# Moving the SBUF addresses of a two-layer kernel's matmul operands to multiples of 2048 bytes

## The chip, the cores and the metric

The kernel runs on one core of one Trainium2 chip. The metric is the device time of one execution in microseconds (us). Three runs of the kernel before took 1174.01, 1175.48 and 1177.17 us; the median is 1175.48 us.

## The reference

1,024 tokens of 512 channels pass two layers, in float32. With `ln` for a layer norm without weights:

```python
xn = ln(x)
x  = x + s4_convolution(xn) + W_down(silu(xn @ W_gate.T) * (xn @ W_up.T))     # 1,376 hidden
xn = ln(x)
x  = x + causal_attention(xn, 32 heads of 128, sequences of 256) @ wo \
       + (xn @ W_base.T + b_base + gated_low_rank_experts(xn))
```

Attention multiplies q and k, masks, takes a softmax over the keys, multiplies by v and projects with wo. It is by far the largest part.

## The kernel before, in words

**Arithmetic.** Float32 accuracy comes from splitting each operand into two float32r tensors, `_hi` and `_lo`. `matmul3` (lines 97 to 101) issues three matmuls into one accumulator: hi by hi (L99), stationary hi by moving lo (L100), stationary lo by moving hi (L101). The first operand of `nc.tensor.matmul` after the output is the stationary one, whose 128 columns are loaded as weights; the second one is moving, up to 512 columns streamed past them. The profile writes the moving operand first: `banks<-xT_hi,wqk_hi` streams `xT_hi` past the weights `wqk_hi`. A stationary slice is 512 bytes of a partition, a moving slice of 512 columns is 2,048.

**Layer 0** (`layer0`, about the first 283 us): `gate_up` runs the gate and up projections in units of 12 matmuls (4 slices of the channels, three matmuls each), weights `gu`, moving `xT`, 22 units for each half of the tokens; `down` has `hT` stationary and `wd` moving; `convolve` has `xT` stationary and `toep` moving; `linear` has `xT` stationary and `wc` moving; `experts` has `hwT` and `wb`. During the first half DVE also computes the convolution's kernel between its tiles, and PE waits for it in places.

**Layer 1** (`attention`, from about 283 us): eight groups of four heads. The order of PE's work is written out in the lists `GROUP` and `LAST_GROUP` and every engine follows it. Its steps: `Q` and `K` (`project`) are one unit of 12 matmuls of 512 columns each, `wqk` stationary, `xT` moving; `V` (`values_or_output`) is such a unit with `xT` stationary and `wv` moving; `W` (in the last group `A` and `B`, 9 and 3 matmuls) has `oT` stationary and `wo` moving; `S` is the scores (L1179 and a `matmul3` of 256 columns, `qT` by `kT`); `T` is three transposes of `prob` (L1188), `O` is `v` by `pT` (256 columns) and L1203. Most Q and K units stand alone between small steps: S, T, unit, O. A group ends with eight W units, seven of them in a row, and begins with S, Q, K. POOL splits the weights (L984, L986) and scales the probabilities (L1002, L1004); ACT and DVE empty the accumulators.

By these lists there are 128 Q and K units: 86 alone after a T, 16 that open a group as the pair Q, K, 8 that follow such a lone unit directly, 16 behind a V unit, 2 issued ahead. There are 64 V units: 38 alone after a T, 24 right behind another V unit, 2 issued ahead.

**Placement.** `place` (line 1224) allocates SBUF tensors one after another at the next multiple of 32 bytes, with no other rule; `late` and `early` blocks are freed and their room used again by what follows. `acc` begins at byte 16,512 of each partition. From the shapes in `build` (lines 1233 to 1261) the first bytes follow; what is left of them modulo 2048 is:

```
acc, xT_hi, xT_lo, ident                                  128
oT, wo, wc_hi, hT, gu, wd, work, toep_hi                  320
qT, kT, v, q_full, k_full, v_full, p_full, pT             320
wc_lo 480; wb, s4, hwT 640; toep_lo 832
wqk_stage, wvo_stage, wqk, wv, prob, tab                 1344
```

(`_hi` and `_lo` alike where not told apart.) Slices inside a tensor begin at multiples of 512 bytes beyond that, except in `wc`, whose rows are 2,600 bytes.

Of the kernel before, what the change touches and what calls it, by code (L numbers as in the profile page):

```python
# [18 lines left out]
P = 128  # L19
F32 = mybir.dt.float32  # L20
# [21 lines left out]
ER = NE * RANK  # L42
WC = DM + ER + NE + 2
CUT = 384
EPS = 1e-5
NEG = -1e30
MAX_THRESHOLD, SCALING = 0.125, 2.0
# [60 lines left out]
def layer0(nc, sem, shared, ins, ffn_sb, expert_sb, small_sb):  # L108
# [77 lines left out]
    def linear_bank(n):  # L186

        return G + 2 * (n % 2) if n < NT - 2 else D + 2 * (n % 2)
# [113 lines left out]
    def scalar_program(act, ahead):  # L302
# [24 lines left out]
        def hg_copy(tiles):  # L327
            for n in tiles:
                half, t = n // TH, n % TH
                act.wait_ge(base_done, n + 1)  # L330
                if half:
                    act.wait_ge(hw_done, 1)
                nc.scalar.activation(hg[:, t, :], banks[:, linear_bank(n) + 1, DM - CUT:WC - CUT],
                                     ACT.Copy).then_inc(hg_done, 1)
# [41 lines left out]
    def vector_program(dve, ahead):  # L376
# [19 lines left out]
        def variance(tiles):  # L396
# [3 lines left out]
            js = slice(tiles[0] % TH, tiles[-1] % TH + 1)  # L400
            nc.vector.tensor_scalar(ln[:, 0, js], mv[:, js, 1], EPS, None, ALU.add).then_inc(var_done, 1)

# [196 lines left out]
        def linear_add(n):  # L599
# [3 lines left out]
            dve.wait_ge(bias_added, n + 1)  # L603
            nc.vector.tensor_tensor(acc[:, t, 0:CUT], acc[:, t, 0:CUT], banks[:, bank, 0:CUT], ALU.add)
            nc.vector.tensor_tensor(acc[:, t, CUT:DM], acc[:, t, CUT:DM], banks[:, bank + 1, 0:DM - CUT],
                                    ALU.add).then_inc(base_added, 1)
# [95 lines left out]
    def tensor_program(pe, ahead):  # L702
# [45 lines left out]
        def linear(n):  # L748
# [5 lines left out]
            if 2 <= n < NT - 2:  # L754
                pe.wait_ge(base_added, n - 1)
            for b, part in ((bank, slice(0, CUT)), (bank + 1, slice(CUT, WC))):
                for k in range(KD):
# [107 lines left out]
def attention(nc, sem, shared, ins, late_sb, attention_sb):  # L865
# [5 lines left out]
    acc, xT_hi, xT_lo, ident, _, banks, y_done = shared  # L871
    w_qk, w_v, w_o, mask_dram, out = ins
    oT_hi, oT_lo, wo_hi, wo_lo = late_sb
    (qT_hi, qT_lo, kT_hi, kT_lo, v_hi, v_lo, q_full, k_full, v_full, p_full, wqk_stage, wvo_stage, wqk_hi, wqk_lo,
     wv_hi, wv_lo, prob, pT_hi, pT_lo, mask, top, total, inv) = attention_sb
    G, S, T, O = 0, 4, 6, 7

    mask_loaded = sem("mask_loaded")
# [342 lines left out]
def build(nc, x, w_gu, w_down, lam, p_ri, q_ri, ct, vc, bp, d_skip, log_step, om_rows, om_cols, tables,  # L1221
          w_comb, b_base, b_thr, w_expb, w_qk, w_v, w_o, identity, mask, out):
    with ExitStack() as ctx:
        def place(stack, *tensors):
            return [stack.enter_context(nc.sbuf_tensor(name, shape, dt)) for name, shape, dt in tensors]

        def split(name, shape):
            return (f"{name}_hi", shape, F32R), (f"{name}_lo", shape, F32R)

        def sem(name):  # L1230
            return ctx.enter_context(nc.semaphore(name))

        acc, xT_hi, xT_lo, ident = place(ctx, ("acc", [P, NT, DM], F32), *split("xT", [P, KD, TOK]),
                                         ("ident", [P, P], F32))
        small_sb = place(ctx, ("vcs", [NS, 2 * NS], F32), ("bps", [NS, NS], F32), ("sm", [NS, 12], F32),
                         ("ex", [NS, 4], F32), ("exi", [NS, 1], mybir.dt.int32), ("bb", [NS, 8], F32),
                         ("vv", [NS, 16], F32), ("omc", [P, 2, KD], F32), ("cs", [P, 12, KD], F32),
                         ("A", [P, KD, 8], F32), ("dsk", [P, 2], F32), ("st", [P, TH, 6], F32),
                         ("mv", [P, TH, 2], F32), ("ln", [P, 4, TH], F32), ("gt", [P, 10, TH], F32))


        with ExitStack() as late:
            late_sb = place(late, *split("oT", [P, GH, TOK]), *split("wo", [P, GH, DM]))
        shared_bytes = 4 * 2 * (GH * TOK + GH * DM)
        expert_bytes = 4 * (2 * KD * WC + 2 * DM + 8 * DM + 2 * TH * P)
        expert_sb = place(ctx, *split("wc", [P, KD, WC]), *split("wb", [P, DM]), ("s4", [P, 8, DM], F32),
                          *split("hwT", [P, TH, P]), ("rest", [P, (shared_bytes - expert_bytes) // 4], F32))
        with ExitStack() as early:
            ffn_sb = place(early, *split("hT", [P, NF, HALF]), ("gu_stage", [P, 2, 2, KD, P], F32),
                           *split("gu", [P, 2, 2, KD, P]), ("wd_stage", [P, 2, DM], F32), *split("wd", [P, 2, DM]),  # L1250
                           ("work", [P, 4, DM], F32), *split("toep", [P, P + DM]),
                           ("tab", [P, KD * WC + DM], F32))
        attention_sb = place(ctx, *split("qT", [P, BATCH, P]), *split("kT", [P, TOK]),
                             *split("v", [P, BATCH, GH * DH]), ("q_full", [P, BATCH, P], F32),
                             ("k_full", [P, BATCH, P], F32), ("v_full", [P, BATCH, GH * DH], F32),
                             ("p_full", [P, 2, P], F32),
                             ("wqk_stage", [P, RING, 2, KD, DH], F32), ("wvo_stage", [P, RING, DM], F32),
                             *split("wqk", [P, RING, 2, KD, DH]), *split("wv", [P, KD, GH * DH]),
                             ("prob", [P, 2, 3 * P], F32),
                             *split("pT", [P, 2, 2 * P]), ("mask", [P, 2 * P], F32),  # L1260
                             ("top", [P, 2, 2], F32), ("total", [P, 2, 2], F32), ("inv", [P, 2, 2], F32))
        banks = ctx.enter_context(nc.psum_tensor("banks", [P, 8, DM], F32))
        shared = (acc, xT_hi, xT_lo, ident, identity, banks, sem("y_done"))

        (sync_0, gpsimd_0, scalar_0, vector_0, tensor_0) = layer0(
            nc, sem, shared, (x, w_gu, w_down, lam, p_ri, q_ri, ct, vc, bp, d_skip, log_step, om_rows, om_cols,
                              tables, w_comb, b_base, b_thr, w_expb), ffn_sb, expert_sb, small_sb)
        (sync_1, gpsimd_1, scalar_1, vector_1, tensor_1, scalar_ahead, vector_ahead, tensor_ahead,
         credits) = attention(nc, sem, shared, (w_qk, w_v, w_o, mask, out), late_sb, attention_sb)

        block = ctx.enter_context(nc.Block())

        @block.sync
        def _(sp):
            sync_0(sp)
            sync_1(sp)

        @block.gpsimd
        def _(pool):
            gpsimd_0(pool)  # L1280
            gpsimd_1(pool)

        @block.scalar
        def _(act):
            scalar_0(act, lambda *part: scalar_ahead(act, *part))
            scalar_1(act)

        @block.vector
        def _(dve):
            credits(dve)  # L1290
            vector_0(dve, lambda *part: vector_ahead(dve, *part))
            vector_1(dve)

        @block.tensor
        def _(pe):
            tensor_0(pe, lambda *part: tensor_ahead(pe, *part))
            tensor_1(pe)
# [72 lines left out]
```

## Time and profile before

| what | value |
|---|---|
| runs | 1174.01, 1175.48, 1177.17 us |
| span of the profiled execution | 1174.2 us, 18,048 instructions |
| PE (matmul) | 1158.9 us busy, 99% of the span, 6,014 instructions |
| PE weight loads | 987.4 us, 84% |
| DVE, ACT, POOL | 44%, 34%, 42% |
| granted TensorE clock, mean | 0.995 |
| DMA | 59.0 MB, 16 engines busy 15.6% |

The page gives no time of its own for the profiled execution beside its span, 1174.2 us; it lies 1.3 us under the median and within the runs. A matmul's busy time in the profile overlaps that of the next, so what PE can deliver is read from the starts of successive matmuls, not from their durations.

### The profile page before, as it was taken

Reading aid. Unit: us, or ns where it says so; the run is one execution under the profiler, and the core shown is the slowest. Engines: PE = TensorE matmul, PEld = TensorE weight load, DVE = VectorE, ACT = ScalarE, POOL = GpSimd, SP = SyncE. Lnnn points to the kernel's source line nnn. Section 1 sums busy time; section 2 is a strip of 40 time slices with the busy share of each in tenths; the row PEclk is TensorE's granted clock in tenths of the full one; section 3 lists DMA queues with packets and bytes.
Section 4 is the critical chain, followed back from the end, with each engine's and each line's share of the span. In section 5 each row is a group of like instructions: output and inputs, shape, how many; then the busy total and the mean of one; then the engine's idle time right before and its main releaser. Section 6 shows DMA issues by size and latency. Waiting matters only on the chain.

```text
span 1174.2 us, 18048 instructions
## 1 busy us (share of the span) xinstructions
PE 1158.9 (99%) x6014; PEld 987.4 (84%) x6014; DVE 513.8 (44%) x1409; ACT 402.8 (34%) x1215; POOL 492.2 (42%) x623
## 2 busy tenths in 40 slices
PE   7989999999999999999999999999999999999998
PEld 6777888898888888888888888888888888888887
DVE  5786256275344334334433343344234423443345
ACT  2321132012363236224513451355135413532351
POOL 3655586671354136323623351346135512642330
PEclk9989999999999999999999999999999999999999
DMA  6222322130021002000200020112001100110001
GB/s 206 90 71 88 120 90 72 46 112 27 19 64 36 27 18 71 27 27 18 89 9 27 18 98 0 36 44 64 1 35 54 53 27 18 63 36 28 10 1 72
DMA packets 24814, 59.00 MB, mean 50 GB/s; under 512 B 3536, under 2 KB 3856, under 8 KB 24656
## 3 DMA queue, kind: packets, MB, share of 16 engines
q1 hardware_dynamic: 24784, 58.61, 15.6%
q8 instruction: 17, 0.28, 0.1%
q14 instruction: 13, 0.11, 0.0%
HBM read 56.50 MB, written 2.10 MB: 50 GB/s over the span
## 4 chain that ended last, share of the span: by engine, by line
PE 93%; DVE 4%; issue 1%; ACT 1%; DMA 0%; POOL 0%; SPq 0%; ACTq 0%; DVEq 0%; POOLq 0%
PE banks L99 28%; PE banks L101 28%; PE banks L100 28%; PE banks L1188 4%; PE banks L1203 2%; PE banks L1179 2%; DVE acc L1112 1%; PE banks L707 0%; DMA acc<-in_x 0%; DVE work L416 0%; DVE vv L505 0%; PE banks L831 0%; DVE s L487 0%; DVE work L441 0%; ACT hT_hi L324 0%
## 5 line engine op out<-in xcount | busy, mean ns | idle before, releaser
L1002 POOL TENSOR_SCALAR prob<-prob,inv 128x128 f32<-128x128 f32 x128 | 48.0, 375 | 550.7 <-DVE inv L1089 550.7
L99 PE MATMUL banks<-xT_hi,wqk_hi 128*128 128x512 f32 x512 | 208.0, 406 | 0.0
L101 PE MATMUL banks<-xT_hi,wqk_lo 128*128 128x512 f32 x512 | 202.2, 395 | 0.0
L100 PE MATMUL banks<-xT_lo,wqk_hi 128*128 128x512 f32 x512 | 200.5, 392 | 0.0
L1061 ACT ACTIVATE prob<-prob,top 128x128 f32<-128x128 f32 (+1 forms) x256 | 114.6, 449 | 192.8 <-DVE top L1099 192.8
L101 PEld LDWEIGHTS banks<-xT_hi,wqk_lo 128*128 128x128 f32 x512 | 96.1, 188 | 21.2
L100 PEld LDWEIGHTS banks<-xT_lo,wqk_hi 128*128 128x128 f32 x512 | 96.7, 189 | 18.5
L99 PEld LDWEIGHTS banks<-xT_hi,wqk_hi 128*128 128x128 f32 x512 | 96.3, 188 | 17.4
L1032 DVE TENSOR_TENSOR kT_lo<-banks,kT_hi 128x512 fp32r<-128x512 f32 x64 | 44.3, 692 | 142.6 <-ACT kT_hi L1027 142.6
L99 PE MATMUL banks<-wv_hi,xT_hi 128*128 128x512 f32 x256 | 104.6, 409 | 0.0
L99 PE MATMUL banks<-wo_hi,oT_hi 128*128 128x512 f32 x256 | 101.6, 397 | 0.0
L101 PE MATMUL banks<-wv_hi,xT_lo 128*128 128x512 f32 x256 | 101.2, 395 | 0.0
L100 PE MATMUL banks<-wv_lo,xT_hi 128*128 128x512 f32 x256 | 101.2, 395 | 0.0
L1112 DVE TENSOR_TENSOR acc<-acc,banks 128x512 f32<-128x512 f32 x72 | 49.4, 687 | 116.6 <-PE banks L101 116.6
L101 PE MATMUL banks<-wo_hi,oT_lo 128*128 128x512 f32 x256 | 100.0, 391 | 0.0
L100 PE MATMUL banks<-wo_lo,oT_hi 128*128 128x512 f32 x256 | 99.6, 389 | 0.0
L1099 DVE CUSTOM_DVE_ANT_0 prob<-banks,mask 128x128 f32<-128x128 f32 (+1 forms) x256 | 80.8, 353 | 14.9 <-PE banks L101 14.5
L986 POOL TENSOR_TENSOR wqk_lo<-wqk_stage,wqk_hi 128x512 fp32r<-128x512 f32 x64 | 83.0, 1297 | 5.3
L99 PE MATMUL banks<-xT_hi,gu_hi 128*128 128x512 f32 (+1 forms) x184 | 72.6, 395 | 2.4 <-DVE xT_lo L433 1.3
L101 PE MATMUL banks<-xT_hi,gu_lo 128*128 128x512 f32 (+1 forms) x184 | 71.8, 390 | 0.0
L100 PE MATMUL banks<-xT_lo,gu_hi 128*128 128x512 f32 (+1 forms) x184 | 71.8, 390 | 0.0
L1074 ACT ACTIVATE p_full<-banks 128x128 f32<-128x128 f32 x128 | 35.6, 278 | 102.4 <-PE banks L1188 95.2
(225 smaller groups left out, 2488.9 us busy)
## 6 DMA issues: line engine op xcount, KB each, us to landing
wqk_stage<-in_w_qk SPq DMA_DIRECT2D x32, 512.0 KB, 3.4
gu_stage<-in_w_gu SPq DMA_DIRECT2D x22, 512.0 KB, 3.4
wvo_stage<-in_w_v SPq DMA_DIRECT2D x32, 256.0 KB, 2.7
wvo_stage<-in_w_o SPq DMA_DIRECT2D x32, 256.0 KB, 2.7
wd_stage<-in_w_down SPq DMA_DIRECT2D x22, 256.0 KB, 2.7
acc<-in_x SPq DMA_DIRECT2D x8, 256.0 KB, 5.9
out<-acc SPq DMA_DIRECT2D x8, 256.0 KB, 2.1
tab<-in_w_comb SPq DMA_DIRECT2D x1, 1300.0 KB, 6.4
```

The costliest lines, as they stand in the source:

```text
L99: nc.tensor.matmul(out, w_hi, x_hi, start=first, stop=False)
L100: nc.tensor.matmul(out, w_hi, x_lo, start=False, stop=False)
L101: return nc.tensor.matmul(out, w_lo, x_hi, start=False, stop=last)
L986: nc.gpsimd.tensor_tensor(lo, src, as_f32(hi), ALU.subtract).then_inc(ready, 1)
L1002: nc.gpsimd.tensor_scalar(prob[:, i, 0:P], prob[:, i, 0:P], inv[:, i, 0:1], 1.0, ALU.mult, ALU.mult)
L1032: nc.vector.tensor_tensor(lo, src, as_f32(hi), ALU.subtract).then_inc(unit_free, 1)
L1061: ins = nc.scalar.activation(pr, pr, ACT.Exp, bias=top[:, p % 2, r:r + 1], scale=-1.0, accum_out=total[:, p % 2, r:r + 1])
L1074: nc.scalar.activation(p_full[:, p % 2], banks[:, T, 2 * P:3 * P], ACT.Copy)
L1099: ins = nc.vector.tensor_tensor_reduce(out=pr, in0=sc, in1=ma, scale=-QK_SCALE, scalar=3e38, op0=ALU.add, op1=ALU.min, accum_out=top[:, p ...
L1112: nc.vector.tensor_tensor(acc[:, t, :], acc[:, t, :], unit_bank(n), ALU.add).then_inc(unit_free, 1)
L1179: nc.tensor.matmul(banks[:, S + n % 2, 0:P], q_full[:, b], k_full[:, b], start=True, stop=True)
L1188: ins = nc.tensor.transpose(banks[:, T, part], prob[:, n % 2, part], ident[:, :])
```

## The change

A constant `LINE = 2048` and a helper that allocates a filler tensor up to the next multiple of 2048 bytes. It is called ahead of `acc` (1,920 bytes) and ahead of `oT` (1,856 bytes). `p_full` (1,024 bytes) moves from before `wqk_stage` to behind `prob` (3,072 bytes). No instruction, order or wait is touched.

```diff
+LINE = 2048
...
+        def line_up(name):
+            start = -(-nc.sbuf_base // 32) * 32
+            place(ctx, (name, [P, -start % LINE // 4], F32))
+
+        line_up("before_acc")
         acc, xT_hi, xT_lo, ident = place(ctx, ("acc", [P, NT, DM], F32), *split("xT", [P, KD, TOK]),
...
+        line_up("before_oT")
...
                              ("k_full", [P, BATCH, P], F32), ("v_full", [P, BATCH, GH * DH], F32),
-                             ("p_full", [P, 2, P], F32),
                              ("wqk_stage", [P, RING, 2, KD, DH], F32), ("wvo_stage", [P, RING, DM], F32),
...
-                             ("prob", [P, 2, 3 * P], F32),
+                             ("prob", [P, 2, 3 * P], F32), ("p_full", [P, 2, P], F32),
```

The remainders modulo 2048 become 0 for `acc`, `xT`, `ident`, `oT`, `wo`, `wc_hi`, `hT`, `gu`, `wd`, `work`, `toep_hi`, `qT`, `kT`, `v`, `q_full`, `k_full`, `v_full`, `wqk`, `wv`, `prob` and `pT`; 160 for `wc_lo`, 320 for `wb`, `s4` and `hwT`, 512 for `toep_lo`, 1024 for `tab` and `p_full`. The last byte used moves from 224,736 to 228,512.

## Rows read from the trace of the kernel before

**Rows 1.** The page: busy time, granted clock in 40 slices, the chain by engine.

```profile
PE 1158.9 (99%) x6014; PEld 987.4 (84%) x6014; DVE 513.8 (44%) x1409; ACT 402.8 (34%) x1215; POOL 492.2 (42%) x623
...
PEclk9989999999999999999999999999999999999999
...
PE 93%; DVE 4%; issue 1%; ACT 1%; DMA 0%; POOL 0%; SPq 0%; ACTq 0%; DVEq 0%; POOLq 0%
```

**Rows 2.** What PE waited for: us in total, times, longest us.

```profile
PE banks L818 <- DVEq L509: 2.5, 1, 2.5
...
PE banks L99 <- DVE work L441: 1.1, 2, 0.6
PE banks L1188 <- POOL prob L1004: 0.4, 1, 0.4
```

**Rows 3.** Groups by line and form: count, busy us, mean ns.

```profile
L99 PE MATMUL banks<-xT_hi,wqk_hi 128*128 128x512 f32 x512 | 208.0, 406 | 0.0
...
L99 PE MATMUL banks<-wv_hi,xT_hi 128*128 128x512 f32 x256 | 104.6, 409 | 0.0
```

**Rows 4.** Timeline (start us, busy us): six W units; down, four chunks.

```profile
603.23 0.39 PE L99 MATMUL banks<-wo_hi,oT_hi 128*128 128x512 f32 x1
...
619.55 0.38 PE L1179 MATMUL banks<-k_full,q_full 128*128 128x128 f32 x2
...
95.43 0.39 PE L99 MATMUL banks<-wd_hi,hT_hi 128*128 128x512 f32 x1
...
106.32 0.28 PE L707 MATMUL banks<-ident,work 128*128 128x128 f32 x1
```

**Rows 5.** Timeline: gate and up, 264 matmuls of half 1, 119 of half 0.

```profile
132.88 0.40 PE L99 MATMUL banks<-xT_hi,gu_hi 128*128 128x512 f32 x1
...
194.48 0.40 PE L99 MATMUL banks<-wd_hi,hT_hi 128*128 128x512 f32 x1
...
25.53 0.40 PE L99 MATMUL banks<-xT_hi,gu_hi 128*128 128x512 f32 x1
...
52.78 0.40 PE L101 MATMUL banks<-xT_hi,gu_lo 128*128 128x512 f32 x1
```

**Rows 6.** Timeline: a V unit after T, from its second matmul, and the next.

```profile
528.62 0.40 PE L100 MATMUL banks<-wv_lo,xT_hi 128*128 128x512 f32 x1
...
531.18 0.39 PE L99 MATMUL banks<-wv_hi,xT_hi 128*128 128x512 f32 x1
...
533.98 0.39 PE L99 MATMUL banks<-xT_hi,wqk_hi 128*128 128x512 f32 x1
```

**Rows 7.** Timeline: Q, K opening a group; a lone Q unit from its second matmul.

```profile
620.13 0.40 PE L99 MATMUL banks<-xT_hi,wqk_hi 128*128 128x512 f32 x1
...
625.73 0.27 PE L1179 MATMUL banks<-k_full,q_full 128*128 128x128 f32 x1
...
552.58 0.39 PE L100 MATMUL banks<-xT_lo,wqk_hi 128*128 128x512 f32 x1
...
555.10 0.28 PE L99 MATMUL banks<-pT_hi,v_hi 128*128 128x256 f32 x1
```

**Rows 8.** Timeline: a W unit after O, second to fourth matmul.

```profile
600.70 0.39 PE L100 MATMUL banks<-wo_lo,oT_hi 128*128 128x512 f32 x1
600.92 0.40 PE L101 MATMUL banks<-wo_hi,oT_lo 128*128 128x512 f32 x1
601.16 0.40 PE L99 MATMUL banks<-wo_hi,oT_hi 128*128 128x512 f32 x1
```

**Rows 9.** Timeline: L1203 behind O, the next T, POOL's last work before it.

```profile
555.46 0.39 PE L1203 MATMUL banks<-p_full,v_full 128*128 128x128 f32 x2
...
556.27 0.49 PE L1188 MATMUL banks<-ident,prob 128*128 128x128 f32 x3
...
554.78 0.48 POOL L1004 TENSOR_SCALAR prob<-prob,inv 128x256 f32<-128x256 f32 x1
```

More of the change, by code:

```diff
@@ L873, in attention @@
     oT_hi, oT_lo, wo_hi, wo_lo = late_sb
-    (qT_hi, qT_lo, kT_hi, kT_lo, v_hi, v_lo, q_full, k_full, v_full, p_full, wqk_stage, wvo_stage, wqk_hi, wqk_lo,
-     wv_hi, wv_lo, prob, pT_hi, pT_lo, mask, top, total, inv) = attention_sb
+    (qT_hi, qT_lo, kT_hi, kT_lo, v_hi, v_lo, q_full, k_full, v_full, wqk_stage, wvo_stage, wqk_hi, wqk_lo,
+     wv_hi, wv_lo, prob, p_full, pT_hi, pT_lo, mask, top, total, inv) = attention_sb
     G, S, T, O = 0, 4, 6, 7
```

## The prediction

> **What bounds the kernel now.** The page comes first: PE is busy 99% of the span, the others under 45%, 93% of the chain that ended last is PE's, and the granted clock is at the upper level, 2.4 GHz, in nearly every slice [rows 1]. The list of waits says the same from the other side: in the attention layer PE waited once, for 0.4 us [rows 2]. So whatever changes the rate at which PE passes from one matmul to the next changes the time, one for one. Most of that rate is in matmuls of 512 columns: three lines of 512 with `wqk` and three of 256 with `wv` [rows 3], 2,304 together.
>
> Their durations are no rate, since they overlap, so I read starts in the timeline. At 2.4 GHz 512 columns are 213.3 ns. No stretch reaches that, and they differ:
>
> - W units, `oT` by `wo`: 72 matmuls from 603.23 to 619.55 us, 226.7 ns each; `hT` by `wd`: 48 from 95.43 to 106.32, 226.9 ns [rows 4].
> - gate and up, `gu` by `xT`: half 1 61.60 us over 264, 233.3 ns; half 0 27.25 us over 119, 229.0 ns [rows 5].
> - V units, `xT` by `wv`: a lone one 2.56 us over its last 11, 232.7 ns; the one behind it 2.80 us over 12, 233.3 ns [rows 6].
> - Q and K opening a group: 5.60 us over 24, 233.3 ns; a lone unit 2.52 us over 11, 229.1 ns [rows 7].
>
> The shape, the clock and the three-matmul pattern are the same in all. What differs is the distance between the places of the two operands that PE reads at once, the stream and the next weights. `oT` and `wo` both lie at remainder 320, `hT` and `wd` too: they run at 226.7. `xT` lies at 128 and its partners at 320 or 1344, which is 192 or 1216 away: none of those stretches settles at 226.7. I take it that the two reads disturb each other by where they stand relative to one another, and that equal remainders let them settle. It is a correlation, over few tensors. A unit does not begin settled: a W unit right behind a small step takes 2.53 us over its last 11 (600.70 to 603.23), 230.0 ns, with spacings up to 0.24 [rows 4, 8]; the units behind it run at 226.7.
>
> **The change, part by part.** The fillers and the moved `p_full` put `xT`, `gu`, `wqk` and `wv` at remainder 0, so all those pairs become equal, as `oT`/`wo` already are. They cost no instruction. Each class of units is then priced by the equal pair in the same position:
>
> - V right behind V, 24 units: 2.80 becomes 12 x 0.2267 = 2.72, 0.08 each, 1.9 us.
> - V alone, 38 units: 2.56 becomes the lone W unit's 2.53, 0.03 each, 1.1 us.
> - The pair Q, K that opens seven of the groups at 233.3 ns (the first group's I leave out): K gains 0.08; Q begins behind a small step, and becomes one slow spacing and a lone unit's 2.53, 2.76, a gain of 0.04. Seven pairs, 0.8 us.
> - Q or K behind a V or behind a lone unit, 24 units. I did not price them by rows of their own but by gate and up of half 0, which has the same distance modulo 1024 between stream and weights: 229.0 to 226.7 is 0.028 a unit, 0.7 us.
> - Q and K alone, 86 units: 2.52 now against 2.53 for a lone equal pair: nothing. This is the largest class, and the rows say that it does not gain, because a unit is over before it has settled.
> - Gate and up of half 1: 61.60 less 264 x 0.2267 = 59.85, 1.8 us.
> - Gate and up of half 0: nothing. Some 0.3 us would be gained before each place where PE waits for DVE (0.6 and 2.5 us at most [rows 2]), and DVE's work there does not move: PE waits longer by what it gains. The convolution (`xT` by `toep`, 24 matmuls of 512 columns) is worth at most 24 x 7 ns, 0.2 us; left out.
> - `linear`: `wc_lo` and every row of `wc` beyond the first stay at other remainders; nothing, with either sign for its 192 shorter matmuls.
> - S and O: `kT` by `qT`, `pT` by `v` are equal already and stay so; nothing. Their three matmuls of 256 columns take 0.36 us (555.10 to 555.46 [rows 7, 9]), where the settled rate would give 0.34.
> - W, `down`, `experts`: equal before and after.
> - The moved `p_full`, the transposes and the DVE, ACT and POOL instructions on new addresses: nothing. The work of the other three is under PE's; POOL ends the probabilities at 555.26, T starts at 556.27 [rows 9], 1.0 us of cover, against 0.03 us that a lone unit may lose or gain. DMAs end in the same order; 15% busy.
>
> Sum: 1.9 + 1.1 + 0.8 + 0.7 + 1.8 = 6.3 us. The profiled span of 1174.2 becomes 1167.9; the median lies 1.3 us over that span, so 1169.2 us, 0.54% less.
>
> Bounds of what is not shown. Below: lone units might settle at once under the new places (124 units x 0.04 = 5 us more), and O's matmuls drop to 0.34 (128 x 0.02 = 2.6 us): 14 us in all, 1161.6. Above: lone Q and K units might run at 233.3 like the openers do now (86 x 11 x 4.2 ns = 4.0 us lost): 1173.2. I take the middle, since the lone W unit is the nearest row.
>
> **A rule of the skill against this.** The rows above show that PE's rate differs between pairs at one clock [rows 4 to 7]. The Trainium skill, TensorE: Matmul & The Clock Gate, section Step-by-step: what each phase is for, says that the stream and the weight load have independent SBUF read ports and that loading the next weights takes no bandwidth from the running matmul. By it places would not matter and the sum would be 0; the trace does not say what else makes 226.7 and 233.3. In SBUF — State Buffer, section Operand start alignment, the skill asks only for multiples of the element size, as a matter of legality, and says that nothing there was timed. The section Back-to-back issue gap of the first page gives N/2.4 + 2.5 ns, 216 ns for 512 columns; the trace has 226.7 at best.
>
> **The rivals.**
>
> *No effect.* `xT` is in every slow pair; something else about it (it lies low in SBUF, it is used as both kinds of operand) may be the cause, and its distance from its partners a coincidence. For: no slow pair without `xT`. Against: with `xT` the same shape runs at 229.0 and 233.3, so it is no fixed property. Time: 1175.5. 10%. This is the case that the rule of two ports in the Trainium skill (TensorE: Matmul & The Clock Gate) describes.
>
> *Never settled.* The equal pairs that settle have run in long unbroken rows; with `xT` they may stay at the lone W unit's 230.0. V, Q, K and gate and up of half 1 are 2,568 matmuls; weighted by their present paces (1,536 at about 229.5, 1,032 at 233.3) they average 231.0, so 2,568 x 1.0 ns = 2.6 us: 1172.9, within 0.3%. Against: `hT` by `wd` settled with 12 matmuls per weight chunk. 5%.
>
> *Slower: both reads on one boundary.* With everything at 0, stream and weights begin together at a 2048-byte boundary, at every matmul; if that is the worst place and not the best, each matmul of these pairs takes the longest spacing in the rows, 0.24 us (600.92 to 601.16 [rows 8]). That is 2,568 x 9 ns = 23 us: 1198.6. It decides from a common pace of 231.0 ns upwards, and is slower by over 0.3% from 232.4. For: a shift to 0 is not among the places the trace shows, only equality at 320. Against: `oT` and `wo` too begin at the same remainder and run best. 7%.
>
> *More than forecast.* Every stream of 2,048 bytes now crosses a 2048-byte boundary, at every remainder in use; if the 13.4 ns over 213.3 come from that crossing, all 512-column matmuls lose them: 2,568 and the 768 of W and 264 of `down`, 3,600 x 13.4 = 48 us beside the 6: 1121. Against: S and O matmuls that cross nothing take 0.12 for 256 columns, not 0.107 [rows 7, 9]. 2%.
>
> **How the numbers follow.** The forecast with its bounds has 76%, centre 1169.2, own range 1161.6 to 1173.2. No effect 10%, never settled 5%, slower 7%, more 2%. What a measurement of this kernel can tell from no change is about 0.3%, 3.5 us, so the line is at 1172.0. Faster: nearly all of the first case and the last, 0.77; same: 0.16, the middle cases and the upper edge of the first; slower: 0.07. The range of 8 in 10 is 1161 to 1175.5: the forecast's own and on to the case of no effect.
>
> **What would show it.** In the profile after: gate and up of half 1 at 59.9 us instead of 61.6 (or at 61.6: no effect); the second V unit of a pair at 2.72; K at the opening of a group at 2.72; lone Q units unchanged at 2.5; W units unchanged at 226.7; the waits for DVE in layer 0 longer by up to 0.6 us in all; nothing new among PE's waits in layer 1. I am wrong if the V and half 1 paces do not fall, if lone units move by more than 0.03 us each (they are 124, so they would rule the sum), or if a 512-column spacing goes under 0.22.

## The result, and the profile after

Four runs of the changed kernel took 1166.81 to 1168.54 us, median 1167.98; four of the kernel before took 1174.01 to 1177.17, median 1175.40. The ratio is 0.9938 [0.9924, 0.9952]: 7.4 us less, 0.6%. The forecast was 1169.2 us in a range of 1161 to 1175.5, faster by over 0.3%; both hold.

The profiled execution has a span of 1165.1 us (1166.81 us by its time, the lowest of the four). Beside the 1174.2 us of before that is 9.1 us, more than the medians give: profiles of one execution each, and one of them at the lower end of its runs. 1.1 us of it lies ahead of the first matmul of 512 columns; the section on the prediction compares that with the other kernels' traces.

The page answers to [rows 1]: busy time, granted clock in 40 slices, the chain by engine.

```profile
PE 1149.5 (99%) x6014; PEld 986.4 (85%) x6014; DVE 514.5 (44%) x1409; ACT 402.9 (35%) x1215; POOL 491.2 (42%) x623
...
PEclk9989999999999999999999999999999999999999
...
PE 94%; DVE 4%; ACT 1%; issue 0%; DMA 0%; SPq 0%; POOL 0%; DVEq 0%; ACTq 0%; POOLq 0%
```

The instructions are the same in number, the clock stands at the same digits in all 40 slices, and PE is still the whole chain. It is busy for 9.4 us less: its matmuls follow one another more closely. What PE waited for, the answer to [rows 2]:

```profile
PE banks L100 <- DVE work L442: 6.3, 2, 5.7
PE banks L708 <- DVE work L417: 2.4, 2, 1.8
PE banks L787 <- DVE toep_lo L390: 1.9, 1, 1.9
PE banks L100 <- DVE xT_lo L434: 1.1, 1, 1.1
PE banks L1189 <- POOL prob L1005: 0.4, 1, 0.4
PE banks L100 <- DVE hwT_lo L645: 0.2, 1, 0.2
```

(Every line number is one higher than before.) In layer 1 the one wait of 0.4 us is still the only one. In layer 0, between the first matmul of 512 columns and the first with `wd`, the waits are 6.3 us instead of 3.6: one of 5.7 us ahead of a gate and up unit, where the same place had 0.6 before, and none at the matmuls of `vv` (2.5 us at L818 before). All waits of this view together are 12.3 us, against 11.9 before; those ahead of that stretch are shorter.

The wait of 5.7 us ends with DVE's work at L442, and DVE comes to it late, because a row of its instructions on `s`, which belongs to the convolution's kernel, takes longer. From the timelines of DVE and POOL (VectorE and GpSimd), before and after; columns are start and busy time in us:

```profile
59.33 0.68 DVE L486 TENSOR_TENSOR s<-s 64x512 f32<-64x512 f32 x1
60.05 3.35 DVE L487 RECIPROCAL s<-s 64x512 f32<-64x512 f32 x1
61.02 2.41 POOL L261 TENSOR_TENSOR gu_lo<-gu_stage,gu_hi 128x1024 fp32r<-128x1024 f32 x1
```

```profile
58.83 1.41 DVE L486 TENSOR_TENSOR s<-s 64x512 f32<-64x512 f32 x1
60.28 2.77 DVE L487 TENSOR_TENSOR s<-s 64x512 f32<-64x512 f32 x1
59.80 2.71 POOL L262 TENSOR_TENSOR gu_lo<-gu_stage,gu_hi 128x1024 fp32r<-128x1024 f32 x1
```

The same instruction (L486 before, L487 after) takes 2.77 us instead of 0.68. POOL splits the next weights there as soon as PE is done with the last ones; relative to DVE's row this now begins 1.5 us sooner. Three TENSOR_TENSOR instructions of the row run beside POOL's work and each ends 0.5 us after it. Before, the split ran beside the reciprocal, which takes 3.35 us in both kernels. DVE's row takes 10.3 us instead of 6.8, and PE waits for it.

The low stretch of the granted clock moved with them. Windows of 10 us; the columns are window, us, busy us (instructions) of PE, weight loads, DVE, ACT and POOL, then the granted clock, DMA share and GB/s. Before:

```profile
70.00:80.00 10.00, 7.49 (x36) 5.91 (x35) 9.35 (x16) 0.60 (x1) 7.18 (x6) 1.00 0.11 27
80.00:90.00 10.00, 10.00 (x37) 8.20 (x37) 6.49 (x43) 1.75 (x3) 0.00 (x0) 0.66 0.09 27
```

After:

```profile
60.00:70.00 10.00, 4.32 (x19) 3.26 (x18) 9.04 (x6) 0.61 (x2) 5.89 (x3) 0.81 0.29 105
70.00:80.00 10.00, 10.00 (x39) 8.11 (x38) 6.69 (x21) 3.65 (x6) 2.96 (x2) 0.85 0.00 0
```

Both times PE was idle for some us, the clock fell to the lower level, 1.2 GHz, for a while, and rose again: before, 0.34 of one window, after, 0.19 and 0.15 of two. The loss is the same 3.4 us of low clock; it only comes earlier.

The starts in the timeline are what counts. Six W units, then gate and up of half 1 (264 matmuls), the answers to [rows 4] and [rows 5]:

```profile
598.47 0.39 PE L100 MATMUL banks<-wo_hi,oT_hi 128*128 128x512 f32 x1
...
614.79 0.27 PE L1180 MATMUL banks<-k_full,q_full 128*128 128x128 f32 x1
...
132.49 0.39 PE L100 MATMUL banks<-xT_hi,gu_hi 128*128 128x512 f32 x1
...
192.36 0.39 PE L100 MATMUL banks<-wd_hi,hT_hi 128*128 128x512 f32 x1
```

W takes 16.32 us over 72 matmuls, 226.7 ns, as before. Half 1 takes 59.87 us over 264, 226.8 ns; it was 61.60, 233.3 ns. The two V units of [rows 6], from the second matmul of the first to the Q unit behind them:

```profile
524.42 0.39 PE L101 MATMUL banks<-wv_lo,xT_hi 128*128 128x512 f32 x1
...
526.96 0.39 PE L100 MATMUL banks<-wv_hi,xT_hi 128*128 128x512 f32 x1
...
529.68 0.39 PE L100 MATMUL banks<-xT_hi,wqk_hi 128*128 128x512 f32 x1
```

2.54 and 2.72 us, where they took 2.56 and 2.80. The K unit that opens a group, and a lone Q unit from its second matmul [rows 7]:

```profile
618.10 0.39 PE L100 MATMUL banks<-xT_hi,wqk_hi 128*128 128x512 f32 x1
...
620.82 0.27 PE L1180 MATMUL banks<-k_full,q_full 128*128 128x128 f32 x1
...
548.03 0.39 PE L101 MATMUL banks<-xT_lo,wqk_hi 128*128 128x512 f32 x1
...
550.56 0.28 PE L100 MATMUL banks<-pT_hi,v_hi 128*128 128x256 f32 x1
```

K takes 2.72 us (2.80 before, half of the pair's 5.60), the lone Q 2.53 (2.52 before). The distances from one matmul to the next in ns show how a unit gets there. A Q unit right behind a T, early in the third group, before and after, from its first matmul:

```
before  316 226 233 236 229 232 226 229 232 225 230 231
after   318 231 236 228 233 230 227 227 226 227 227 226
```

After the change the sequence ends in 227, 227, 226 and stays there until the next small step; before, a 226, 229, 232 goes on without end. A V unit before ends in a 231, 236 without end.

**Where the time went**, by the starts of the same matmuls in both traces (us, before to after; these are sums or stretches of the whole trace):

```
start of the first 512-column matmul      25.53  ->  24.44    -1.1
gate and up of half 0, to the first wd    64.45  ->  65.15    +0.7
gate and up of half 1                     61.60  ->  59.87    -1.7
the other stretches of layer 0                                -0.1
layer 1, from its first S to the end      891.5  ->  884.7    -6.9
  of that: V -3.8, Q and K -2.5, O -0.2, S -0.2, W -0.2 (V, Q and K with
  the few units that are issued ahead of layer 1)
span                                     1174.2  -> 1165.1    -9.1
```

### The profile page after: what moved, and what is told of

It is laid out like the page before. It is cut to its first block, busy times and chain, and to the rows that moved or that the text cites. A ratio compares the mean times of both kernels' runs of the same rounds, so it can differ in the third digit from the quotient of the medians.

```text
span 1165.1 us, 18048 instructions
## 1 busy us (share of the span) xinstructions
PE 1149.5 (99%) x6014; PEld 986.4 (85%) x6014; DVE 514.5 (44%) x1409; ACT 402.9 (35%) x1215; POOL 491.2 (42%) x623
## 4 chain that ended last, share of the span: by engine, by line
PE 94%; DVE 4%; ACT 1%; issue 0%; DMA 0%; SPq 0%; POOL 0%; DVEq 0%; ACTq 0%; POOLq 0%
PE banks L100 28%; PE banks L102 28%; PE banks L101 28%; PE banks L1189 4%; PE banks L1204 2%; PE banks L1180 2%; DVE acc L1113 1%; PE banks L708 0%; DMA acc<-in_x 0%; DVE work L417 0%; PE banks L832 0%; DVE s L488 0%; DVE hT_lo L445 0%; DVE s L487 0%; DVE work L442 0%
```

## The experiments

The trace of after agrees with the distance between the two operands as the cause, but the change moved several things at once: `xT` went to a multiple of 2048, its partners did too, the distance became 0, and `p_full` moved. The candidates that could be told apart by places alone were: the distance, with a period to be found; the absolute place of `xT` (the rival of no effect, in another form: something about `xT` alone); and the boundary at 2048 bytes as a thing of its own, for better or worse. The run at 320 and those at five other distances set the fillers through one more argument, the remainder that they fill up to:

```diff
-        def line_up(name):
+        def line_up(name, rest=0):
             start = -(-nc.sbuf_base // 32) * 32
-            place(ctx, (name, [P, -start % LINE // 4], F32))
+            place(ctx, (name, [P, (rest - start) % LINE // 4], F32))
```

The unit that all of them are read by is the second of two V units early in the third group (at about 515 us), 12 matmuls, and gate and up of half 1. That V unit of after:

```profile
513.02 0.39 PE L100 MATMUL banks<-wv_hi,xT_hi 128*128 128x512 f32 x1
...
515.74 0.28 PE L100 MATMUL banks<-pT_hi,v_hi 128*128 128x256 f32 x1
```

2.72 us; in the kernel before it took 2.80.

### Equal remainders elsewhere than at 0

```diff
-        line_up("before_acc")
+        line_up("before_acc", 320)
...
-        line_up("before_oT")
+        line_up("before_oT", 320)
```

> All tensors that the change puts at remainder 0 of 2048 lie at remainder 320 here, so no matmul operand of 512 columns begins on a 2048-byte boundary, but the stream and the weights still have equal remainders. Theory (what counts is the distance of the two operands from each other): the same as the change, about 1168 us, gate and up of half 1 at 226.7 ns a matmul (59.9 us for 264), the second V unit of a pair at 2.72 us. Rival (what counts is that an operand begins on a multiple of 2048 bytes): the old paces, 233.3 ns and 2.80 us, about 1175 us.

1168.98 us, ratio 0.9942 [0.9929, 0.9956]. The timeline of this kernel, the V unit:

```profile
513.27 0.39 PE L100 MATMUL banks<-wv_hi,xT_hi 128*128 128x512 f32 x1
...
515.99 0.28 PE L100 MATMUL banks<-pT_hi,v_hi 128*128 128x256 f32 x1
```

2.72 us, and half 1 59.86 us. No operand begins at a multiple of 2048 here, and all of the gain is there: over all units V takes 178.75 us and Q and K 358.90, as in the changed kernel (178.72 and 358.90). The multiple of 2048 does nothing.

### Only the first filler

The second call of `line_up` is taken out and `p_full` is back in its old place. `xT` lies at 0, and everything behind it shifts with it, so all distances are those of before.

```diff
-        line_up("before_oT")
...
+                             ("p_full", [P, 2, P], F32),
                              ("wqk_stage", [P, RING, 2, KD, DH], F32), ("wvo_stage", [P, RING, DM], F32),
...
-                             ("prob", [P, 2, 3 * P], F32), ("p_full", [P, 2, P], F32),
+                             ("prob", [P, 2, 3 * P], F32),
```

> Only the filler ahead of acc: acc and xT begin at a multiple of 2048 bytes, and all that follows is shifted with them, so that every distance between two tensors is that of the kernel before. Theory (distance): the paces of before, 233.3 ns for gate and up of half 1, 229 ns for half 0, 2.80 us for the second V unit, about 1175.4 us. Rival (boundaries): the stream of gate and up, Q and K, which is xT, now begins on a boundary, so these gain at least in part, 1 to 4 us less than before; V, which streams wv, does not.

1176.41 us, ratio 1.0001 [0.9984, 1.0017]. Its timeline, the V unit and half 1:

```profile
518.04 0.39 PE L100 MATMUL banks<-wv_hi,xT_hi 128*128 128x512 f32 x1
...
520.84 0.28 PE L100 MATMUL banks<-pT_hi,v_hi 128*128 128x256 f32 x1
...
133.87 0.40 PE L100 MATMUL banks<-xT_hi,gu_hi 128*128 128x512 f32 x1
...
195.47 0.40 PE L100 MATMUL banks<-wd_hi,hT_hi 128*128 128x512 f32 x1
```

2.80 and 61.60 us: the kernel before, to the hundredth. All V units take 182.50 us, all Q and K 361.46 (182.52 and 361.42 before). `xT` at a multiple of 2048 is worth nothing by itself. With the run above this makes the distance the cause: there the distance was 0 away from every such multiple, here `xT` is on one at the old distance, and the time follows the distance both times.

### The small buffer back in its old place

Both fillers stay; the two lines of `p_full` are undone as above. `wqk` and `wv` then begin at 1024, `xT` at 0.

> Both fillers, but p_full in its old place, so that wqk and wv lie at remainder 1024 and xT at 0, and layer 0 is as in the change. Theory with a period of 1024 bytes or less in the distance: as the change, about 1168 us, second V unit 2.72 us. Theory with a period of 2048 bytes: layer 0 as in the change, V, Q and K as before or at another pace of their own, second V unit 2.75 to 2.83 us, about 1171 to 1174 us.

1169.11 us, ratio 0.9942 [0.9929, 0.9956]. Its V unit:

```profile
515.32 0.39 PE L100 MATMUL banks<-wv_hi,xT_hi 128*128 128x512 f32 x1
...
518.04 0.28 PE L100 MATMUL banks<-pT_hi,v_hi 128*128 128x256 f32 x1
```

2.72 us; V in all 178.71, Q and K 358.90. A distance of 1024 is as good as 0, and the moved buffer was not needed.

### Other distances: 256, 64, 128, 32, 224

`xT` stays at 0, and everything behind the second filler lies at another remainder. The pairs inside that part (`oT` and `wo`, `hT` and `wd`, `kT` and `qT`) stay equal, so W is an inner control. The edit is the same each time, with the number of the title:

```diff
-        line_up("before_oT")
+        line_up("before_oT", 256)
```

> xT at remainder 0, gu, wqk, wv and toep at 256. With a distance of 64 bytes Q and K ran in the 231/236 ns pattern that V had before at stream minus weights = 1216, and V in the 226/229/232 pattern that Q and K had at minus 192. 1216 is minus 64 and minus 192 is plus 64 modulo 256: the period of the distance is 256 bytes or less. Theory (period 256): as the change, 226.7 ns in long rows, second V unit 2.72 us, about 1168 us. Rival (the period is longer and the match above is chance): other paces, 229 ns or more, above 1171 us.

1167.78 us, ratio 0.9944 [0.9931, 0.9957]. Its V unit:

```profile
513.81 0.39 PE L100 MATMUL banks<-wv_hi,xT_hi 128*128 128x512 f32 x1
...
516.53 0.28 PE L100 MATMUL banks<-pT_hi,v_hi 128*128 128x256 f32 x1
```

2.72 us. 256 bytes apart is as good as 0.

> The change with the second filler aimed at remainder 64: xT at 0, gu, wqk, wv, toep at 64; W, down, S and O stay equal pairs. Theory: a distance of 64 bytes is unequal, and gate and up, V, Q and K run above 226.7 ns when in long rows; half 1 between 229 and 236 ns, total 1172 to 1180 us. If the period is 64 bytes or less (the distance of before is 192, a multiple of 64, and was not equal), it would be as the change; the rows of before speak against that.

1175.98 us, ratio 0.9999 [0.9989, 1.0008]. Its V unit, and a lone Q unit from its second matmul:

```profile
516.84 0.39 PE L100 MATMUL banks<-wv_hi,xT_hi 128*128 128x512 f32 x1
...
519.59 0.28 PE L100 MATMUL banks<-pT_hi,v_hi 128*128 128x256 f32 x1
...
547.97 0.40 PE L101 MATMUL banks<-xT_lo,wqk_hi 128*128 128x512 f32 x1
...
550.54 0.28 PE L100 MATMUL banks<-pT_hi,v_hi 128*128 128x256 f32 x1
```

V 2.75 us, Q 2.57: V is better than before by 0.05, Q worse by 0.05. All V units take 179.59 us (2.9 less than before) and all Q and K 366.14 (4.7 more): the total is that of before, but by two effects that largely cancel. The reason is in the sign. Before, V's stream lies 1,216 bytes above its weights, which is -64 modulo 256, and in Q and K the roles are swapped, +64; here it is the other way round. The distances in ns from one matmul to the next, in a V unit behind another and in Q and K units:

```
before          V  231 236 231 236 231 235 ...     Q, K  226 229 232 226 229 232 ...
distance 64     V  232 226 229 231 226 229 ...     Q, K  236 231 236 231 236 230 ...
```

The patterns change places with the sign. It is not the whole rule: gate and up of half 1 before had the distance of Q and K and yet ran at 233.3 ns, and so did the opening Q and K, while half 0 had 229.0. So what ran just before seems to decide too which pattern a row falls into; a run with half the weight columns, further down, bears on this.

Each of the next three kernels was executed once.

> xT at 0, its partners at 128, half of the supposed period of 256 bytes. By a period of 256 the distance is the same in either direction, so V, Q and K should share one pattern; I expect it between 229 and 236 ns, since it is farthest from equal, total 1170 to 1182 us. By a period of 128 or less it would be as the change, 226.7 ns; that is spoken against by plus 64 and minus 64 giving different patterns.

1176.59 us, with 1174.87 for the kernel before on the same chip. Its V unit:

```profile
516.88 0.39 PE L100 MATMUL banks<-wv_hi,xT_hi 128*128 128x512 f32 x1
...
519.65 0.28 PE L100 MATMUL banks<-pT_hi,v_hi 128*128 128x256 f32 x1
```

2.77 us; V in all 181.64, Q and K 363.84. In long rows V, Q and K, and gate and up of half 1 all share one pattern here, as the theory had it:

```
distance 128    V  230 233 241 232 231 232 228 ...     Q, K  230 233 241 232 231 232 228 ...
```

That is 232.4 ns on average: at half the period it is nearly, but not quite, as bad as elsewhere.

> xT at 0, its partners at 32. Tells whether a distance under 64 bytes counts as equal. If the unit is 64 bytes: as the change, second V unit 2.72 us, half 1 at 226.7 ns. If each 32 bytes count: Q, K and half 1 lie between the equal pattern (226.7) and that of minus 64 (233.4), V between 226.7 and 229.1.

1174.03 us. Its V unit:

```profile
512.38 0.40 PE L100 MATMUL banks<-wv_hi,xT_hi 128*128 128x512 f32 x1
...
515.18 0.28 PE L100 MATMUL banks<-pT_hi,v_hi 128*128 128x256 f32 x1
```

2.80 us; V in all 182.28, Q and K 365.70. That the whole is 0.8 us under the kernel before, though V and Q and K together take 4 us more than there, comes from layer 0. The first matmul of 512 columns begins at 20.92 us there, before at 25.53; the waits listed in this execution are 8.2 us instead of 11.9, and the windows from 70 to 90 us have a granted clock of 0.87 and 0.96, a loss of 1.7 us, half of what it was before and after. So the total of a single execution says little here, and the units are what to read. 32 bytes, the least step that `place` makes, already cost V as much as the distance of before does. The expectation was wrong in this: it had V between 226.7 and 229.1 ns, and V takes 233.3.

> xT at 0, its partners at 224, which is minus 32 modulo 256. If the period is 256 and each 32 bytes count, V takes here the pattern that Q and K have at 32 and the other way round. If the unit is 64 bytes, the pattern is that of 192 or of 256: Q and K 229.1 and V 233.4 ns, or both 226.7.

1178.62 us. Its V unit:

```profile
517.56 0.40 PE L100 MATMUL banks<-wv_hi,xT_hi 128*128 128x512 f32 x1
...
520.36 0.28 PE L100 MATMUL banks<-pT_hi,v_hi 128*128 128x256 f32 x1
```

2.80 us; V in all 182.36, Q and K 365.22. 224 is -32 modulo 256, so by a period of 256 V should take the pattern that Q and K have at 32, and the other way round. In ns:

```
distance 32     V  235 234 234 231 235 233 ...     Q, K  232 235 231 235 232 235 ...
distance 224    V  235 232 235 231 235 232 ...     Q, K  233 234 231 235 234 234 ...
```

That is what is there.

The table of all, us, the distance being that from `xT` to its partners modulo 256:

```
distance        V units, all 64    Q and K, all 128    gate and up half 1
0   (after)         178.72             358.90               59.87
0   (at 320)        178.75             358.90               59.86
0   (1024)          178.71             358.90               59.86
0   (256)           178.72             358.90               59.86
32                  182.28             365.70               61.61
64                  179.59             366.14               61.60
128                 181.64             363.84               61.34
192 (before)        182.52             361.42               61.60
224                 182.36             365.22               61.60
```

### Is it the amount of weights read? Half the stationary columns

An obvious mechanism for the settled 226.7 ns over the 213.3 of the columns, and for what unequal places cost, is that the weight load takes turns from the stream. If so, half the weight columns should cost half. V, W, A and B load 64 columns instead of 128, in the kernel before and in the changed one; the kernels leave out the other 64 rows of those outputs. Each was executed once.

```diff
+        cols, bank = slice(cols.start, cols.start + P // 2), unit_bank(u)[0:P // 2]
         for k in heads:
-            ins = matmul3(nc, unit_bank(u), left[0][:, k, cols], left[1][:, k, cols],
+            ins = matmul3(nc, bank, left[0][:, k, cols], left[1][:, k, cols],
```

> The kernel before with 64 instead of 128 stationary columns in V, W, A and B units: the other 64 rows of their outputs are left out, the streams stay 512 columns. It halves the weight reads beside the stream. If the loss of an unequal pair comes from weight reads that meet the stream, the second V unit, 233.3 ns a matmul with 6.6 ns over the equal pair, falls to about 230 ns or less (2.72 to 2.77 us a unit). Rival (the loss belongs to the stream alone and depends on its own place): 233.3 ns stays. W units, equal: 226.7 if the 13.4 ns over 213.3 belong to the stream; about 220 if they belong to the weight reads.

> The changed kernel with the same 64 stationary columns in V, W, A and B units. V and W are equal pairs. If the 13.4 ns over 213.3 in settled rows belong to the stream, the second V unit and the W units stay at 226.7 ns (2.72 us a unit); if to the weight reads, both are at about 220 ns (2.64 us). A lone V unit, 2.53 us over its last 11 matmuls, falls towards 2.49 if its transient comes from weight reads.

1175.61 us (kernel before on that chip: 1175.6) and 1172.64 us. In the variant of the changed kernel, six W units, and the V unit:

```profile
601.87 0.39 PE L100 MATMUL banks<-wo_hi,oT_hi 128*64 128x512 f32 x1
...
618.42 0.27 PE L1181 MATMUL banks<-k_full,q_full 128*128 128x128 f32 x1
...
516.21 0.40 PE L100 MATMUL banks<-wv_hi,xT_hi 128*64 128x512 f32 x1
...
518.97 0.28 PE L100 MATMUL banks<-pT_hi,v_hi 128*128 128x256 f32 x1
```

W takes 16.55 us over 72, 229.9 ns, where full weights take 226.7; V 2.76 us, 230 ns. In the variant of before, V 2.79 us (517.23 to 520.02), hardly less than 2.80, and W is slower as well, 16.57 us (603.15 to 619.72).

For equal pairs halving the load took nothing away: they are slower by 3.3 ns, where 226.7 or about 220 was expected, and lose the steady pace. The distances in W are now 230 236 229 224 227 234, over and over. So the 13.4 ns between 213.3 and 226.7 aren't a price per weight byte. But what an unequal place costs does depend on the load. Over all V units the kernel before falls from 182.5 to 181.3 us and the changed one rises from 178.7 to 180.0: the difference between the two shrinks from 3.8 to 1.2 us, half by unequal pairs that got faster and half by equal ones that got slower.

The variant of before also shows what the history of a row does. Its Q and K units are not edited and lie where they lay, but the K unit that opens a group falls from 2.80 to 2.75 us and from the distances 233 233 234 to 226 229 232, with other V and W units ahead of it.

The cost of an unequal place looks like a matter of the moment at which the load meets the stream, and a shorter load shifts that moment as another address does. That last sentence is an argument from these patterns, no measurement.

### The rest of the tensors, too

`wc` has rows of 2,600 bytes, so of its eight slices one alone began at 0 after the change. Its rows are widened from 650 to 768 elements, at the cost of the unused tensor behind, and `wc_lo`, `wb`, `s4` and `hwT` come to 0 with it.

```diff
+WCP = 768
...
-        expert_sb = place(ctx, *split("wc", [P, KD, WC]), *split("wb", [P, DM]), ("s4", [P, 8, DM], F32),
-                          *split("hwT", [P, TH, P]), ("rest", [P, (shared_bytes - expert_bytes) // 4], F32))
+        expert_sb = place(ctx, *split("wc", [P, KD, WCP]), *split("wb", [P, DM]), ("s4", [P, 8, DM], F32),
+                          *split("hwT", [P, TH, P]))
```

> The change with rows of wc widened from 650 to 768 elements in SBUF, so that every row of wc_hi and wc_lo, and wb, s4 and hwT, begin at remainder 0. linear's 96 matmuls of 384 columns take 17.0 us and its 96 of 266 columns 11.9 us in the changed kernel by their starts; at 17/16 cycle a column they would take 16.3 and 11.3. Theory (distance modulo 256): between 0.3 and 1.2 us less than the change, since each length begins unsettled; in total 1167 to 1168 us, not to be told from the change. If rows already at other remainders cost nothing: 17.0 and 11.9 us stay.

1168.39 us, ratio 0.9943 [0.993, 0.9956]: not to be told from the changed kernel. The last six tiles of `linear` in its timeline:

```profile
240.78 0.42 PE L101 MATMUL banks<-wc_hi,xT_hi 128*128 128x384 f32 x1
...
262.15 0.39 PE L101 MATMUL banks<-xT_hi,wqk_hi 128*128 128x512 f32 x1
```

That is 21.37 us, against 21.69 in the changed kernel (240.67 to 262.36 us). All of `linear`'s matmuls together go down by 0.4 us, which is within what was expected and which the total can't show. No variant was found that is measurably faster than the changed kernel.

## Why the prediction was right, point by point

**What bounds the kernel.** PE's pace, one for one: right in layer 1 and in half 1. PE's busy time fell by 9.4 us and the span by 9.1. In half 0 a faster PE had to wait longer than it gained, as the last of the terms shows.

**The cause.** Taken from a correlation over few tensors, with the remark that it was one; the runs at 320, with the first filler alone and at five distances make it shown. What the prediction did not have is the period: it spoke of equal remainders modulo 2048, and priced `wqk` at 1216 as far from `xT`. The rule is the distance modulo 256: 0, 256 and 1024 are equal, 32 is not.

**The terms.**

- V behind V, 24 units: 1.9 us forecast, 67.20 to 65.28 us, 1.92 measured.
- V alone, 38 units: 1.1 forecast, 109.63 to 107.88, 1.75 measured. From their second matmul on, lone V units took 2.57 us on average before and 2.52 after; the forecast went from one row of 2.56 to the lone W unit's 2.53. This is the largest term that was mis-sized, and 0.046 us a unit is beyond the 0.03 that the prediction named as a sign of being wrong, though all 124 lone units together moved by 0.019 each. A hundredth of a microsecond in one row is 0.4 us here.
- The opening pairs and the 24 units behind others: 1.5 forecast. All units there that aren't lone went down by 1.95.
- Q and K alone, 86 units: 0 forecast, 244.67 to 244.08, 0.59 measured, 7 ns each. The single rows (2.52 before, 2.53 after) even point the other way; only the sum over the class shows it.
- Half 1: 1.8 forecast, 1.73 measured.
- O, S and W: 0 forecast with a bound of 2.6 us for O, 0.6 measured, 0.24 of it O.
- `linear`, the convolution and the other stretches: 0 forecast, 0.1 measured.
- Half 0: 0 forecast, by the reason that DVE's work does not move and PE waits longer by what it gains, up to 0.6 us. That step failed. The stretch was 0.7 us longer and its waits 2.7 us, because DVE's row on `s` took 10.3 us instead of 6.8. It is no chance of one execution: in the six kernels with distance 0 DVE's row takes 10.3 to 10.4 us, the waits of the stretch are 6.3 and the stretch 65.1 to 65.8 us; in the three with the distances of before they are 6.8, 3.4 to 3.6, and 64.3 to 64.5 us, and at the four other distances DVE's row takes 6.8 too. So the change costs 0.7 us or more in half 0, through a collision of DVE with POOL that a faster PE brings about.

The sum over layer 1 was 4.5 us and came out at 6.9, by 0.65 for lone V, 0.6 for lone Q and K, 0.6 for the small steps and 0.45 for the pairs and the units behind others. Half 0 took back 0.7. Without the start the trace thus gives 8.0 us for the forecast 6.3, and the medians give 7.4; the forecast of 1169.2 lies 1.2 us above the median. It came that close in part by luck: the layer 1 terms were 2.4 us too small, and half 0 was missed the other way.

**The start.** The profile of after has its first input in place sooner (`acc<-in_x` from issue to landing: 4.8 us against 5.9). In the eleven other kernels, whose first instructions are the same, this was 4.6 to 5.7 us, and 4.6 in one with all tensors placed as before. The first matmul of 512 columns began at 24.2 to 26.4 us with distance 0 and at 25.5 to 26.7 with the distances of before. So the 1.1 us vary by themselves at least in great part. They are most of the 1.7 us by which the two profiles stand further apart than the medians; the rest is within the spread of single executions, 1.7 us for the changed kernel and 3.2 for the one before.

**The rivals.** *No effect* fell with the result, and with the first filler alone, which gave just that time: the place of `xT` is nothing. *Never settled* fell at half 1, 226.8 ns, and at the V unit behind another; a lone unit settles after some seven matmuls. *Slower on one boundary* and *more than forecast* both fell with the result, 226.7 ns and neither 240 nor 213.3, and the run at 320 has the same pace: at equal remainders the boundary makes no difference of either sign. The place "from which it decides", a common pace over 231.0 ns, was missed by 4 ns.

**The rule against it.** The Trainium skill, TensorE: Matmul & The Clock Gate, section Step-by-step: what each phase is for, gives the stream and the weight load independent read ports, so that a load takes nothing from a running matmul. By it no place could matter. Here 0.6% of the kernel hangs on the places alone, at one clock and with the same instructions; the measurement decides. How the two disturb each other stays open: the runs with half the load exclude that the 13.4 ns are in proportion to what is loaded, though they show that the load's size changes what an unequal place costs, and nothing run here separates the load's timing from the way in which SBUF serves the two reads.

## What to carry to other kernels

Where matmuls run in long rows on one engine, put the tensors that are read together, the stream and the next weights, at equal remainders modulo 256 bytes; in this kernel two fillers of under 2 KB in each partition gave 0.6%, and neither the absolute place nor a coarser multiple mattered. To see the pace in a profile, take the starts of matmuls of one shape in several stretches and compare their pace. Durations do not show it (0.39 to 0.40 us for both paces), and a class of a hundred short units must be priced by its sum, since a hundredth of a microsecond in a single row is the size of the effect. Then look at what the faster engine sets off: here POOL's splits came sooner, met DVE's row and took 0.7 us of the gain back.

## What was not expected of the hardware

- The sign of the distance counts: at +64 and -64 bytes a row of matmuls of 512 columns takes different patterns, 226 229 232 ns and 231 236 ns, and V and Q and K swap theirs when the sign does. The same distance can also give either pattern (half 0 of before at 229.0 ns, half 1 at 233.3), so the history of a row counts as well; the K unit that opens a group changed its pattern when only units ahead of it were edited.
- 32 bytes apart is fully unequal: 233 ns or so, like 224.
- Loading half as many weights slowed equal pairs from 226.7 to 229.9 ns a matmul, and shrank what the unequal places cost in all V units from 3.8 to 1.2 us.
- A TENSOR_TENSOR of DVE that takes 0.68 us alone took 1.41 and 2.77 us beside POOL's split of weights and ended 0.5 us after it; a RECIPROCAL that ran beside the same work took 3.35 us before and after.
- The best pace seen is 226.7 ns for 512 columns, at each of the four ways to make the distance 0, 13.4 ns above the 213.3 of the columns. No run took any of that away, and what it is stays open.
